# A graph attention layer on one core: scores a group earlier, exponents in three buffers, copied weights in two

## The chip, the cores and the metric

The kernel runs on one core of a Trainium2 chip. The metric is the time of one execution on the device in microseconds; of the kernel before there are three runs, 1566.85 to 1569.98 us, and one profiled execution.

## What is computed

x is 4096 x 128. Four layers of a graph network follow each other, each as x = x + layer(relu(layernorm(x)), adj), with one adjacency matrix of 4096 x 4096 that is almost empty. The change touches the last layer alone:

```python
attn = jnp.einsum('nhc,mhc->hnm', q, k) / np.float32(np.sqrt(C))     # H = 4 heads, C = 32
neg = jnp.where(adj == 0.0, -jnp.inf, attn)
m = jnp.max(neg, axis=-1, keepdims=True)
e = jnp.exp(neg - m)                                                 # 0 where all are masked
alpha = e / jnp.sum(e, axis=-1, keepdims=True)
out = jnp.einsum('hnm,mhc->hnc', alpha, v)
out = beta * x_r + (1.0 - beta) * out                                # beta: a gate from out and x_r
```

## The kernel before

The first layer's pass over the adjacency matrix lists, for every tile of 128 rows, the columns that aren't empty. The other layers work on *groups* of 128 rows and 512 such columns (`Quad`): group q has its buffer b = q % 6 and its turn in a loop that is written out six times (`each_quad`, L369 to L375). The last layer runs 48 groups; a group of another row tile is rescaled and added by an online softmax (`cap`, `capped3`).

For a group, these steps are made, each by one engine:
- SP (`load_adj`, L502 to L516) loads the list, the mask and the queries of group g+5, once DVE has read all scores of group g-1.
- POOL (`gather_nodes`, L685 and L695 on) gathers 512 rows of keys and values in four indirect DMAs for group g+5, once the values of group g-1 are done: `pool.wait_ge(pv_done[k], g.q + 2)`, where the semaphore starts at 2.
- PE turns the keys (`turn_rows`, L1706), 4 transposes; ACT copies them (`keys`, L878) to one buffer kT.
- PE makes the scores (`scores`, L1716): four products of 32 rows each, one a head, into PSUM banks 1 to 4. DVE masks them and takes the maxima (`scores`, L1380, then `maxima3`, L1388 to L1390).
- ACT makes the exponents (`exps3`, L893), four instructions, one a head, in place in `e`.
- PE turns the exponents (`turn_exps`, L1725) in four chunks c of 128 columns, four transposes a chunk; even chunks into bank 5 and copied by ACT (`turned3`, L899), odd ones into bank 6 and copied by DVE (`turned3`, L1396), to `eT`.
- PE multiplies by the values (`values`, L1735): 16 products into bank 7, which show as 32 records and as many weight loads; the last one raises `pv_done`.
- ACT copies the result (`outputs3`, L905), once `pv_done` says so; PE turns it back (`turn_outputs`, L1742); DVE rescales the sum and adds (`add_up3`, L1408 to L1413).

Nothing but the order written in each engine's `step3` decides what runs when. An engine works in order, so a step that waits holds all behind it. In step g PE makes: chunks 2 and 3 of group g, scores of g+2, values of g, chunks 0 and 1 of g+1, keys of g+3, outputs of g. `e` has two buffers and `eT` one. Ahead of the loop stand the first groups' steps (L1753 on for PE); behind it DVE waits for the last exponents and then finishes the layer (`finish3`).

## Time and profile before

| | before |
|---|---|
| median of 3 runs | 1568.05 us (1566.85 to 1569.98) |
| profiled execution | 1554.0 us, span 1552.3 us |
| busy in the span | PE 65%, DVE 58%, POOL 50%, ACT 49% |
| mean granted clock of TensorE | 0.815 of full speed |
| last layer's loop | from about 1176 to 1511 us of the span |

The busy shares are means over four layers with different limits; only the last fifth of the span is in question here. Matmul ends are modelled, so the moment at which a product is really done is read from the engine that waits for it. "remote" and "issue" name waits for which the profile has no other engine's instruction.

### The profile page before, as it was taken

How to read it: one execution, taken by the hardware profiler on the slowest of the kernel's cores; microseconds unless marked ns; L12 is line 12 of the kernel's file. 1: busy time of each engine (PE TensorE's matmuls, PEld its weight loads, DVE VectorE, ACT ScalarE, POOL GpSimd, SP SyncE). 2: the span in 40 equal slices, each digit the busy share in tenths (PEclk: the TensorE clock that was granted, in tenths of full speed). 3: DMA queues.
4: the chain of work that ended last, by engine and by line, in shares of the span. 5: the costliest groups of instructions: out<-in, count | busy, mean ns of one | idle time of the engine just before them, and what ended most of it. 6: DMA issues, size and time to landing. Idle time of an engine off the chain costs nothing.

```text
span 1552.3 us, 29120 instructions
## 1 busy us (share of the span) xinstructions
PE 1006.1 (65%) x6426; PEld 631.8 (41%) x6426; DVE 895.8 (58%) x2430; ACT 756.1 (49%) x3228; POOL 768.8 (50%) x791
## 2 busy tenths in 40 slices
PE   4696858888974515545554286981746777777770
PEld 1353524544542314434443243441524554555440
DVE  3494855986886235544555750103436777777778
ACT  4997666678741313323333250000625666676762
POOL 3007766764555256555655505665054555555550
PEclk9797979898986556665766688996868999999995
DMA  8546656874512444554445876855242445333462
GB/s 272 194 192 227 223 182 180 257 230 166 208 40 64 122 129 101 104 100 94 109 104 98 95 245 224 301 186 62 82 134 79 106 97 105 97 105 100 101 89 58
DMA packets 124455, 219.73 MB, mean 142 GB/s; under 512 B 37350, under 2 KB 93290, under 8 KB 118762
## 3 DMA queue, kind: packets, MB, share of 16 engines
q0 software_dynamic: 25984, 60.45, 21.8%
q1 hardware_dynamic: 83050, 74.24, 15.4%
q10 hardware_dynamic: 15360, 84.43, 14.3%
q14 instruction: 47, 0.39, 0.1%
q8 instruction: 14, 0.23, 0.1%
HBM read 182.18 MB, written 33.18 MB: 139 GB/s over the span
## 4 chain that ended last, share of the span: by engine, by line
DVE 30%; issue 22%; PE 18%; another core or an unknown queue 13%; DVEq 6%; ACT 3%; DMA 3%; SPq 1%; ACTq 1%
DVE work L1380 4%; DVE work L1114 4%; PE ps L1673 3%; PE ps L1716 3%; DVE work L1115 2%; PE ps L1725 2%; PE ps L1526 2%; DVEq L418 1%; DVE work L1051 1%; DVE work L1048 1%; DVE work L1396 1%; DVEq L322 1%; DMA work<-adj_table 1%; PE ps L1522 1%
## 5 line engine op out<-in xcount | busy, mean ns | idle before, releaser
L685 POOL DMA_INDIRECT work<-h_table,stage x304 | 290.6, 956 | 258.8 <-issue 124.9
L801 ACT ACTIVATE unread<-work 128x128 bf16<-128x128 f32 x1024 | 301.0, 295 | 40.8 <-DVE work L1119 16.5
L685 POOL DMA_INDIRECT work<-kv_table,stage x212 | 201.5, 951 | 222.3 <-PE ps L1735 120.5
L642 POOL DMA_INDIRECT work<-in_adj_rows,adj_stage x184 | 238.4, 1296 | 82.6 <-issue 57.0
L1568 PE MATMUL ps<-work,h_wide 128*128 128x512 f32 x512 | 248.5, 641 | 25.5 <-ACT h_wide L732 18.3
L801 ACT ACTIVATION_READ_ACCUMULATOR unread<-work 128x1 f32 x1024 | 191.5, 187 | 7.3 <-issue 6.9
L1380 DVE CUSTOM_DVE_ANT_0 work<-ps,work 128x512 f32<-128x512 f32 x200 | 141.7, 748 | 76.5 <-remote 40.9
L1568 PEld LDWEIGHTS ps<-work,h_wide 128*128 128x128 f32 x512 | 103.7, 208 | 153.7 <-issue 144.8
L1725 PE MATMUL ps<-ident,work 128*128 128x128 f32 x776 | 116.9, 284 | 43.5 <-DVE work L1396 25.1
L893 ACT ACTIVATE work<-work 128x512 f32<-128x512 f32 x197 | 139.8, 713 | 3.5 <-DVE work L1389 2.9
L1648 PE MATMUL ps<-work 128*128 128x128 f32 x384 | 85.9, 394 | 68.9 <-ACT work L842 52.3
L1725 PEld LDWEIGHTS ps<-ident,work 128*128 128x128 f32 x776 | 86.6, 143 | 64.8 <-DVE work L1396 34.7
L1735 PE MATMUL ps<-work 128*32 128x128 f32 x1536 | 79.2, 277 | 49.0 <-issue 48.6
L1648 PEld LDWEIGHTS ps<-work 128*128 128x128 f32 x384 | 75.0, 291 | 78.3 <-ACT work L842 40.8
L1550 PE MATMUL ps<-work 128*32 128x128 f16 x1024 | 67.8, 419 | 49.9 <-DVE work L1051 44.4
L633 POOL COPY adj_stage<-adj_flat 128x4 int32 x46 | 20.8, 452 | 157.6 <-issue 145.2
L1673 PE MATMUL ps<-work,h_wide 128*128 128x512 f32 x192 | 90.9, 614 | 6.4 <-issue 5.1
L1641 PE MATMUL ps<-ident,work 128*128 128x128 f32 x192 | 42.9, 363 | 75.3 <-ACT work L830 40.8
L1735 PEld LDWEIGHTS ps<-work 128*32 128x32 f32 x1536 | 49.1, 109 | 103.4 <-issue 99.3
L1246 DVE TENSOR_REDUCE work<-ps 128x1 f32<-128x512 f32 x49 | 33.9, 692 | 84.3 <-remote 56.6
L1396 DVE COPY work<-ps 128x512 f32<-128x512 f32 x97 | 66.7, 688 | 15.7 <-issue 10.0
L829 ACT ACTIVATE work<-work 128x1 f32<-128x1 f32 x49 | 9.9, 203 | 133.7 <-DVE work L1250 83.9
(216 smaller groups left out, 1802.4 us busy)
## 6 DMA issues: line engine op xcount, KB each, us to landing
work<-in_adj_rows ACTq DMA_DIRECT2D x38, 2048.0 KB
work<-adj_table SPq DMA_DIRECT2D x76, 256.0 KB
work<-in_adj_rows SPq DMA_DIRECT2D x6, 2048.0 KB
adj_table<-work SPq DMA_DIRECT2D x96, 128.0 KB
mask_table<-work SPq DMA_DIRECT2D x53, 128.0 KB
work<-mask_table SPq DMA_DIRECT2D x53, 128.0 KB
work<-h_table,stage POOLq DMA_INDIRECT x304
kv_table<-work SPq DMA_DIRECT2D x32, 128.0 KB
```

The source lines that it names most:

```text
L642: nc.gpsimd.indirect_dma_start(out=ag[:, h, c, :], out_offset=None, in_=adj_rows, in_offset=bass.IndirectOffsetOnAxis(ap=adj_stage[:, h // ...
L685: nc.gpsimd.indirect_dma_start(out=rows[:, b, c, :], out_offset=None, in_=table, in_offset=bass.IndirectOffsetOnAxis(ap=stage[:, b, c:c + ...
L801: ins = nc.scalar.activation(unread[:, m % (MQ // 2) * TB + t, :], ring[:, q, m, t * P:(t + 1) * P], ACT.Abs, accum_out=seen[:, b, t, q * ...
L893: nc.scalar.activation(e[:, b % 2, h, :], e[:, b % 2, h, :], ACT.Exp, bias=nbest3[:, b, h:h + 1], scale=SCALE, accum_out=part3[:, b, h:h + ...
L1380: nc.vector.tensor_tensor_reduce(out=e[:, b % 2, h, :], in0=ps[:, 1 + h, :], in1=mk[:, b, :], scale=1.0, scalar=capped3[:, b, h:h + 1], op ...
L1396: nc.vector.tensor_copy(eT[:, c, :, :], ps[:, 6, :].rearrange("p (h n) -> p h n", h=H)).then_inc(eT_outd, 1)
L1550: ins = mm(ps[NC * g:NC * g + NC, 7 if j % 2 else 3, 0:P], coded[:, j % 2, 0, :, m], onehot[:, j % 2, :, m], start=(m < 4), stop=(m >= T - 4))
L1568: ins = mm(ps[:, 0, :], h_sb[:, q * MQ + m, :], ring[:, q, m, :], start=(q + m == 0), stop=False)
L1648: ins = mm(ps[:, 4 + b % 4, 0:P], eT[:, c, 0, :], hg1[:, b, c, 0:P], start=(c == 0), stop=(c == QC - 1))
L1673: ins = mm(ps[:, 4 + nb, :], h_sb[:, m, :], ring2[:, q, m % MQ, :], start=(m == 0), stop=(m == T - 1))
L1725: ins = nc.tensor.transpose(ps[:, 5 + c % 2, h * P:(h + 1) * P], e[:, b % 2, h, c * P:(c + 1) * P], ident[:, :])
L1735: ins = mm(ps[C * h:C * h + C, 7, 0:P], kvg[:, b, c, P + C * h:P + C * h + C], eT[:, c, h, :], start=(c == 0), stop=(c == QC - 1))
```

## The change

The scores run three groups ahead instead of two, with head 0 of a fourth; the exponents have three buffers (`e_of`), the copied chunks two (`eT_of`); the chunks are made in the order 1, 0, 3, 2 (`turn_place`). PE waits for each head's bank by itself, not for all four. The semaphore `pv_read` gets two more counts at the start, and waits on it are shifted by as much. The loads of SP and the gathers of POOL stay as they were. Before the loop, one group more is scored. The diff, without its unchanged lines:

```diff
--- before.py
+++ after.py
@@ -178,7 +178,10 @@
...
         e1 = e[:, :, 0, :]
+        e_third = work[:, 18688:20224].rearrange("p (h m) -> p h m", h=H - 1)
+        e_third_last = work[:, 8192:8704]
         eT = work[:, 12800:14848].rearrange("p (c h n) -> p c h n", c=QC, h=H)
+        eT_other = work[:, 6144:8192].rearrange("p (c h n) -> p c h n", c=QC, h=H)
         kT = work[:, 14848:15360]
@@ -299,6 +302,7 @@
...
             primed += [pv_done[k], pv_done[k], pv_read[k], pv_read[k], state_reset[k]]
+        primed += [pv_read[3], pv_read[3]]
         for k in (1, 3):
@@ -413,6 +417,17 @@
...
             eng.wait_ge(ag_full[h], 32 * i + (64 if h % 2 else 32))
+
+        def e_of(g, h):
+            n = g.b % 3
+            if n < 2:
+                return e[:, n, h, :]
+            return e_third[:, h, :] if h < H - 1 else e_third_last
+
+        def eT_of(g):
+            return eT_other if g.b % 2 else eT
+
+        turn_place = {1: 0, 0: 1, 3: 2, 2: 3}
@@ -882,21 +897,21 @@
...
                 act.wait_ge(mx_ready[3], g.q + 2)
-                wait(act, pv_read[3], g.q)
+                act.wait_ge(pv_read[3], g.q + 1)
                 nc.scalar.activation(alpha3[:, g.b, :], grown3[:, g.b, :], ACT.Exp, scale=SCALE).then_inc(al_ready[3], 1)
...
                 act.wait_ge(mx_ready[3], q + 2)
-                wait(act, pv_read[3], q)
+                act.wait_ge(pv_read[3], q + 1)
                 for h in heads:
-                    nc.scalar.activation(e[:, b % 2, h, :], e[:, b % 2, h, :], ACT.Exp, bias=nbest3[:, b, h:h + 1],
+                    nc.scalar.activation(e_of(g, h), e_of(g, h), ACT.Exp, bias=nbest3[:, b, h:h + 1],
                                          scale=SCALE, accum_out=part3[:, b, h:h + 1]).then_inc(e_ready[3], 1)
...
             def turned3(g, c):
-                act.wait_ge(eT_done[3], QC * g.q + c + 2)
-                act.wait_ge(pv_done[3], g.q + 2)
-                nc.scalar.activation(eT[:, c, :, :], ps[:, 5, :].rearrange("p (h n) -> p h n", h=H),
+                act.wait_ge(eT_done[3], QC * g.q + turn_place[c] + 2)
+                act.wait_ge(pv_done[3], g.q + 1)
+                nc.scalar.activation(eT_of(g)[:, c, :, :], ps[:, 5, :].rearrange("p (h n) -> p h n", h=H),
                                      ACT.Copy).then_inc(eT_out[3], 1)
@@ -905,22 +920,25 @@
...
             def step3(g):
+                exps3(g.ahead(1), (0,))
+                rescale(g)
                 turned3(g, 2)
-                exps3(g.ahead(1), (1, 2, 3))
-                rescale(g.ahead(1))
+                exps3(g.ahead(2), (3, 2))
+                turned3(g.ahead(1), 0)
+                keys(g.ahead(4))
+                exps3(g.ahead(2), (1,))
                 outputs3(g)
-                turned3(g.ahead(1), 0)
-                keys(g.ahead(3))
-                exps3(g.ahead(2), (0,))
...
             keys(Quad(0, 1))
-            exps3(Quad(0, 0), range(H))
-            rescale(Quad(0, 0))
+            exps3(Quad(0, 0), (3, 2))
+            keys(Quad(0, 2))
+            exps3(Quad(0, 0), (1, 0))
+            exps3(Quad(0, 1), (3, 2))
             turned3(Quad(0, 0), 0)
-            keys(Quad(0, 2))
-            exps3(Quad(0, 1), (0,))
+            keys(Quad(0, 3))
+            exps3(Quad(0, 1), (1,))
             each_quad(act, step3)
@@ -1367,17 +1385,17 @@
...
-            def scores(g):
+            def scores(g, heads):
                 q, b = g.q, g.b
-                if not isinstance(q, int):
-                    dve.wait_ge(eT_done[3], QC * q - QC + 1)
-                adj_loaded(dve, 3, g, turns3)
-                dve.wait_ge(cap_ready, q + 2)
-                for h in range(H):
+                if 0 in heads:
+                    wait(dve, eT_done[3], QC * q - 2 * QC + 1)
+                    adj_loaded(dve, 3, g, turns3)
+                    dve.wait_ge(cap_ready, q + 2)
+                for h in heads:
                     dve.wait_ge(s_done, H * q + h + 2)
                     settle(dve)
-                    nc.vector.tensor_tensor_reduce(out=e[:, b % 2, h, :], in0=ps[:, 1 + h, :], in1=mk[:, b, :], scale=1.0,
+                    nc.vector.tensor_tensor_reduce(out=e_of(g, h), in0=ps[:, 1 + h, :], in1=mk[:, b, :], scale=1.0,
                                                    scalar=capped3[:, b, h:h + 1], op0=ALU.subtract, op1=ALU.max,
@@ -1391,9 +1409,9 @@
...
             def turned3(g, c):
-                dve.wait_ge(eT_done[3], QC * g.q + c + 2)
-                dve.wait_ge(pv_done[3], g.q + 2)
-                nc.vector.tensor_copy(eT[:, c, :, :], ps[:, 6, :].rearrange("p (h n) -> p h n", h=H)).then_inc(eT_outd, 1)
+                dve.wait_ge(eT_done[3], QC * g.q + turn_place[c] + 2)
+                dve.wait_ge(pv_done[3], g.q + 1)
+                nc.vector.tensor_copy(eT_of(g)[:, c, :, :], ps[:, 6, :].rearrange("p (h n) -> p h n", h=H)).then_inc(eT_outd, 1)
@@ -1412,7 +1430,7 @@
...
                                         ALU.add).then_inc(pv_read[3], 1)
-                dve.wait_ge(pv_read[3], q + 3)
+                dve.wait_ge(pv_read[3], q + 5)
                 settle(dve)
@@ -1468,10 +1486,11 @@
...
             def step3(g):
-                turned3(g, 3)
-                scores(g.ahead(2))
-                maxima3(g.ahead(2))
+                scores(g.ahead(3), (0,))
                 turned3(g.ahead(1), 1)
+                scores(g.ahead(3), (1, 2, 3))
+                turned3(g.ahead(1), 3)
+                maxima3(g.ahead(3))
                 add_up3(g)
@@ -1486,12 +1505,18 @@
...
             for b in range(2):
-                scores(Quad(0, b))
+                scores(Quad(0, b), range(H))
                 maxima3(Quad(0, b))
+            scores(Quad(0, 2), (0,))
             turned3(Quad(0, 0), 1)
+            scores(Quad(0, 2), (1, 2, 3))
+            turned3(Quad(0, 0), 3)
+            maxima3(Quad(0, 2))
             end = Quad(each_quad(dve, step3, turns3), 0)
-            dve.wait_ge(e_ready[3], H * end.q + H + 3)
+            dve.wait_ge(e_ready[3], H * end.q + 2 * H + 1)
+            dve.wait_ge(eT_out[3], 2 * end.q + 2)
+            dve.wait_ge(eT_done[3], QC * end.q + QC + 1)
             settle(dve)
@@ -1706,12 +1731,13 @@
...
-            def scores(g):
+            def scores(g, heads):
                 q, b = g.q, g.b
-                adj_loaded(pe, 3, g, turns3)
-                pe.wait_ge(kT_out, q + 2)
-                pe.wait_ge(s_read, H * q + 1)
-                for h in range(H):
+                if 0 in heads:
+                    adj_loaded(pe, 3, g, turns3)
+                    pe.wait_ge(kT_out, q + 2)
+                for h in heads:
+                    wait(pe, s_read, H * q + h - 2)
                     rows = slice(C * h, C * h + C)
@@ -1722,39 +1748,42 @@
...
                     for h in range(H):
-                        ins = nc.tensor.transpose(ps[:, 5 + c % 2, h * P:(h + 1) * P], e[:, b % 2, h, c * P:(c + 1) * P],
+                        ins = nc.tensor.transpose(ps[:, 5 + c % 2, h * P:(h + 1) * P], e_of(g, h)[:, c * P:(c + 1) * P],
                                                   ident[:, :])
...
                 q, b = g.q, g.b
-                pe.wait_ge(pv_read[3], q + 2)
+                pe.wait_ge(pv_read[3], q + 4)
                 for c in range(QC):
...
                     for h in range(H):
-                        ins = mm(ps[C * h:C * h + C, 7, 0:P], kvg[:, b, c, P + C * h:P + C * h + C], eT[:, c, h, :],
+                        ins = mm(ps[C * h:C * h + C, 7, 0:P], kvg[:, b, c, P + C * h:P + C * h + C], eT_of(g)[:, c, h, :],
                                  start=(c == 0), stop=(c == QC - 1))
...
                 pe.wait_ge(oT_out, g.q + 2)
-                pe.wait_ge(pv_read[3], g.q + 2)
+                pe.wait_ge(pv_read[3], g.q + 4)
                 nc.tensor.transpose(ps[:, 7, P:2 * P], outT[:, :], ident[:, :]).then_inc(o_done, 1)
...
             def step3(g):
-                turn_exps(g, (2, 3))
-                scores(g.ahead(2))
+                scores(g.ahead(3), (1, 2, 3))
+                turn_exps(g.ahead(1), (1, 0))
+                turn_rows(g.ahead(4))
                 values(g)
-                turn_exps(g.ahead(1), (0, 1))
-                turn_rows(g.ahead(3))
+                turn_exps(g.ahead(1), (3, 2))
+                scores(g.ahead(4), (0,))
                 turn_outputs(g)
...
             turns3 = turns_of(pe)
-            for b in range(2):
+            for b in range(3):
                 turn_rows(Quad(0, b))
-                scores(Quad(0, b))
-            turn_rows(Quad(0, 2))
-            turn_exps(Quad(0, 0), (0, 1))
+                scores(Quad(0, b), range(H))
+            turn_exps(Quad(0, 0), (1, 0))
+            turn_rows(Quad(0, 3))
+            turn_exps(Quad(0, 0), (3, 2))
+            scores(Quad(0, 3), (0,))
             each_quad(pe, step3, turns3)
```

PE's loop before: one step, from chunks 2 and 3 (L1725) over the scores (L1716) and values (L1735) to the keys (L1706) and outputs (L1742).

```order
265 L1725 MATMUL ps<-ident,work 128x128 x8
266 L1712 REGISTER_ALU
267 L1713 ISA
268 L1716 MATMUL ps<-work 128x512 x4
269 L1735 MATMUL ps<-work 32x128 x8
270 L1733 REGISTER_ALU
271 L1735 MATMUL ps<-work 32x128 x8
272 L1720 REGISTER_ALU
273 L1723 ISA
274 L1725 MATMUL ps<-ident,work 128x128 x8
275 L1706 MATMUL ps<-ident,work 128x128 x4
276 L1742 MATMUL ps<-ident,work 128x128
```

The values stand right behind the four scores, ahead of the chunks of the next group and the keys.

PE's loop after the change, from the registers behind the scores of heads 1 to 3: chunks (L1751), keys (L1731), values (L1761), chunks, score of head 0 (L1742), outputs (L1768).

```order
319 L1749 ISA
320 L1751 MATMUL ps<-ident,work 128x128 x8
321 L1731 MATMUL ps<-ident,work 128x128 x4
322 L1761 MATMUL ps<-work 32x128 x8
323 L1759 REGISTER_ALU
324 L1761 MATMUL ps<-work 32x128 x8
325 L1749 REGISTER_ALU
326 L1751 MATMUL ps<-ident,work 128x128 x8
327 L1738 REGISTER_ALU
328 L322 ISA
329 L1742 MATMUL ps<-work 128x512
330 L1768 MATMUL ps<-ident,work 128x128
```

Eight turned chunks and four keys have moved between the scores and the values, and one score has been taken from the others and stands behind the values.

DVE's loop after the change, the end of a step: the copy of chunk 3 (L1414), the maxima (L1406 to L1408) and the beginning of the addition (L1426).

```order
958 L1414 COPY work<-ps 128x512
959 L1406 TENSOR_TENSOR work<-work 128x4
960 L1407 TENSOR_SCALAR work<-work 128x4
961 L1408 ISA
962 L1408 TENSOR_SCALAR work<-work,cap 128x4
963 L433 REGISTER_ALU
964 L433 TENSOR_LOAD quad_tile
965 L433 ISA x2
966 L1424 REGISTER_ALU
967 L1426 ISA
968 L1426 TENSOR_TENSOR work<-work 128x132
```

Before, the maxima came ahead of the copy of chunk 1, and the addition behind that; the scores and the copy of chunk 3 stood at the step's beginning.

## Rows read from the trace of the kernel before

**Rows 1.** Windows view of the last layer's loop (start:end; length; busy us of each engine)
```profile
1200.00:1500.00 300.00, 226.10 (x2566) 152.75 (x2565) 218.82 (x671) 205.63 (x547) 159.06 (x169) 0.99 0.45 101
```

**Rows 2.** Timeline of PE: first and last value products (start us, us, engine, line)
```profile
1176.34 0.93 PE L1735 MATMUL ps<-work 128*32 128x128 f32 x21
...
1509.73 1.08 PE L1735 MATMUL ps<-work 128*32 128x128 f32 x32
```

**Rows 3.** Waits view, 1200 to 1500: total us, times, longest
```profile
POOL work L685 <- PE ps L1735: 101.4, 42, 2.7
...
PE ps L1725 <- DVE work L1396: 21.7, 34, 1.6
```

**Rows 4.** Lines view by form, 1200 to 1500: busy us, mean ns | idle before, what ended it
```profile
L1380 DVE CUSTOM_DVE_ANT_0 work<-ps,work 128x512 f32<-128x512 f32 x168 | 119.3, 748 | 43.8 <-remote 32.4 <-PE ps L1716 7.6 <-issue 3.6
...
L1396 DVE COPY work<-ps 128x512 f32<-128x512 f32 x84 | 57.8, 688 | 12.9 <-issue 9.2 <-PE ps L1725 3.0 <-DVE work L1413 0.7
```

**Rows 5.** Timeline of POOL: first and last gathers of two groups
```profile
1306.33 0.95 POOL L685 DMA_INDIRECT work<-kv_table,stage  x1 [2.52 <-PE ps L1735]
...
1310.08 0.94 POOL L685 DMA_INDIRECT work<-kv_table,stage  x1 [0.30 <-issue]
...
1334.59 0.95 POOL L685 DMA_INDIRECT work<-kv_table,stage  x1 [2.36 <-PE ps L1735]
1337.43 0.95 POOL L685 DMA_INDIRECT work<-kv_table,stage  x1 [1.90 <-issue]
...
1339.93 0.95 POOL L685 DMA_INDIRECT work<-kv_table,stage  x1 [0.30 <-issue]
```

**Rows 6.** Timeline of ACT: outputs copy, which waits for the values
```profile
1305.38 0.28 ACT L905 ACTIVATE work<-ps 128x128 f32<-128x128 f32 x1 [1.64 <-PE ps L1735]
...
1312.62 0.28 ACT L905 ACTIVATE work<-ps 128x128 f32<-128x128 f32 x1 [1.66 <-PE ps L1735]
...
1333.80 0.28 ACT L905 ACTIVATE work<-ps 128x128 f32<-128x128 f32 x1 [1.53 <-PE ps L1735]
...
1341.93 0.28 ACT L905 ACTIVATE work<-ps 128x128 f32<-128x128 f32 x1 [2.54 <-remote]
```

**Rows 7.** Timelines of PE and its loads, two groups
```profile
1308.91 1.14 PE L1716 MATMUL ps<-work 32*128 32x512 f32 x8
1309.98 1.06 PE L1735 MATMUL ps<-work 128*32 128x128 f32 x27
...
1312.13 0.46 PE L1735 MATMUL ps<-work 128*32 128x128 f32 x4 [0.46 <-issue]
...
1313.45 0.60 PE L1706 MATMUL ps<-ident,work 128*128 128x128 f32 x4
1313.88 0.27 PE L1742 MATMUL ps<-ident,work 128*128 128x128 f32 x1
...
1309.98 0.80 PEld L1735 LDWEIGHTS ps<-work 128*32 128x32 f32 x28 [0.76 <-issue]
...
1337.28 1.14 PE L1716 MATMUL ps<-work 32*128 32x512 f32 x8
1338.35 1.08 PE L1735 MATMUL ps<-work 128*32 128x128 f32 x32
```

**Rows 8.** Source view of the mask load on SP: duration ns min/median/max
```profile
L514 SPq FUSED_REGOPS  x42: 18/458/704, 1201.9 to 1494.4; - x42
```

**Rows 9.** Timelines of DVE and PE ahead of the first values
```profile
1170.71 0.75 DVE L1380 CUSTOM_DVE_ANT_0 work<-ps,work 128x512 f32<-128x512 f32 x1 [2.06 <-remote]
...
1172.25 0.16 DVE L1388 TENSOR_TENSOR work<-work 128x4 f32<-128x4 f32 x1
...
1172.54 0.68 DVE L1396 COPY work<-ps 128x512 f32<-128x512 f32 x1
...
1174.32 2.09 PE L1716 MATMUL ps<-work 32*128 32x512 f32 x8
```

## The prediction

> **What bounds the kernel now.** The change touches the loop of the last layer alone, so I read that stretch. The windows view gives busy times there: of 300 us PE is busy 226.10, DVE 218.82, ACT 205.63, POOL 159.06 [rows 1]. No engine is full, so waits set the pace. The first value products of the 48 groups start at 1176.34 and the last group's at 1509.73 [rows 2], so a group takes 333.4 / 47 = 7.09 us. The diff suggests that engines wait for each other: PE waits 21.7 us for DVE's copies (L1396) and DVE 7.6 us for score products, over 42 groups [rows 3, 4]. That is 0.7 us a group together. The largest wait is another: POOL waits 101.4 us for the value products (L1735), 42 times, 2.4 in the mean and never over 2.7, and DVE waits 32.4 us for something "remote" in front of its scores [rows 3, 4].
>
> So I laid POOL's gathers beside the end of the value products, which is seen as the start of ACT's L905, since ACT waits for just that. At 1305.38 ACT sees the values of a group done; POOL's four gathers start from 1306.33 to 1310.08; the next values are done at 1312.62. From values to first gather 0.95, three steps of 1.25, and 2.54 from the fourth gather to the next values [rows 5, 6]. The reader should see that the last interval hardly depends on PE: when POOL was late by 1.6 us (second gather at 1337.43 where 1334.59 + 1.25 = 1335.84 was due, fourth at 1339.93), PE had issued the scores at 1337.28 and all 32 value products by 1339.43, and yet the values were done only at 1341.93, 2.00 after the fourth gather [rows 5 to 7]. In the ordinary group PE stops in the middle of the values, with 27 of 32 product records issued, for about a microsecond; it goes on at 1312.13, 2.05 after the fourth gather [rows 7]. SP, which does nothing for PE, slows in the same stretch: its register instruction before the mask load takes 18 ns at best and 458 in the median [rows 8]. I read this as **a hold**: while a group's gathers are in flight, completions of PE's products come through late, and about 2.0 us after the fourth gather starts they are let go. POOL in turn starts the next gathers only once the values are done. That closes a ring: 0.87 (0.95 and 0.79 seen, the latter from 1333.80 to 1334.59) + 3.75 + 2.5 = 7.1 us, the 7.09 measured. Mean by the waits view: the four gathers last 4 x 1.25 - 0.30 = 4.70 and POOL's wait is 2.41, together 7.11 [rows 3, 5].
>
> Of contention the Trainium skill says the opposite (SBUF — State Buffer, "Who interferes with whom"): DMA never contends with a compute engine, and PE never waits on anyone. The trace doesn't agree, as far as completions of PE go, since values and gathers move together [rows 5 to 7]. By that rule there is no hold and the loop is bound by the engines' own waits; that is the third case below.
>
> **The change, part by part.**
> *POOL and its wait.* Nothing moves: gather(g+5) still waits for the values of group g-1, four gathers a group. The ring keeps 0.87 + 3.75.
> *PE's order.* Before: exponents' chunks 2, 3; all four scores; values; chunks 0, 1; keys. Now: scores of heads 1 to 3; chunks 1, 0 of the next group; keys; values; chunks 3, 2; the score of head 0; outputs. The number of products is the same. Four heads issued together take 1.07 us until the values follow (1308.91 to 1309.98) [rows 7], as they use different row groups; a head alone costs one head's two passes, the same 1.07. The split adds 1.07 us of PE a group. PE's own need was 1.07 scores + 1.07 values + 21 transposes (16 of exponents, 4 of keys, 1 of outputs) x 0.11 = 4.4 (0.11: 4 keys from 1313.45 to 1313.88) [rows 7]; it is now 5.5. The ring leaves 7.1, so this lies beside it, but with 1.6 us of slack where there were 2.7.
> The Trainium skill speaks against this part too (TensorE: Matmul & The Clock Gate, "Why this matters for your kernels"): a product of 32 rows alone takes as long as one of 128, and the gain is in running four at once. The trace shows the four at once; that one alone costs as much is my reading of it.
> *DVE's and ACT's order.* The same instructions in another order. The buffers (three for exponents, two for the transposed) remove PE's wait for DVE's copy, 21.7 / 42 = 0.5 us, and DVE's for scores, 0.2 [rows 3, 4]. I cost this at nothing: the ring covers it. PE comes to its values earlier, and the hold is late next.
> *From hold to values done.* This is the term that can change. After the hold the value products still queued behind it must run: 2.54 - 2.05 = 0.5 us [rows 5 to 7]. Lower bound: all have run under cover, as at 1341.93, 2.00 after the fourth gather: -0.5 a group. Upper bound: between the first held score and the last value there now stand also 8 turned chunks and 4 keys (24 loads and products). PE stopped before with 27 products and 28 loads of the values issued [rows 7]; if it stops because only so many instructions may stand behind a held one, with 24 more in front some 24 fewer are issued, which is 3 of the 8 steps of 0.13 (1.07 / 8): +0.4. The nearest row is the ordinary group, which had its values partly queued as the new order will (0); the late group had them all (-0.5), but its scores had come through before its second gather could hold them. From 0 I go a quarter of the way to the upper bound, +0.1: 48 x 0.1 = +4.8 us.
> *Prologue.* Three groups are scored before the first values, not two, and group 1 must be turned too. DVE gets free of the gathers at 1170.71, and the first values start at 1176.34 [rows 2, 9]. Added to that chain: 4 scores x 0.75 + maxima 0.3 = 3.3 on DVE and one score pass on PE, 1.07 at full clock, 2.0 at half, as there (2.09) [rows 9]. Sum 4.4 to 5.4; the turned chunks add 8 x 0.11 = 0.9, and some of all this will find cover. I take +5 (3 to 7).
> *End.* Behind the last values now come copy 3, the maxima and only then the addition: 0.69 + 0.3 [rows 4, 9], +1.
> *Sum:* 4.8 + 5 + 1 = +10.8 us. The profiled execution took 1554.0 us (span 1552.3); it becomes 1564.8. The median of the runs, 1568.05, lies 14 us above it; I add the difference to the median: **1578.9 us**. A measurement of this kernel can tell about 0.2%, 3.1 us.
>
> **The rivals.**
> *1, forecast: the ring holds, values end 2.5 to 2.8 behind the fourth gather.* Chance 0.46; own range 1571 to 1593 (0 to +0.4 a group, which is 0 to +19, and 3 to 8 for both ends).
> *2, the ring holds but the rest behind the hold vanishes.* PE is early enough that all values have run when the hold ends: 2.0 instead of 2.5. -0.5 x 48 + 6 = -18: 1550. For it: 1341.93, with everything issued. Against: there are more completions between. Chance 0.22.
> *3, there is no hold; the engines' waits bound, as the diff supposes.* Then the period falls to the fullest engine plus its gaps: by their busy times over 42 groups [rows 1], ACT 4.9, DVE 5.2, PE 5.4 and 1.07 for the split score, 6.5, less what its records overlap: about 6.2, so -0.9 x 48 + 6 = -37: 1531. For it: PE's and DVE's waits above. Against: the values that kept to the gathers [rows 5 to 7]. Chance 0.10.
> *4, slower by much: the hold costs more marks.* Seven completions of PE (three heads, two chunks, the keys, the values) now fall behind the start of the hold; before it was five. Single ones slip through about 0.7 us apart (SP's step at its worst, 704 ns [rows 8]). If even one more of them has to pass before the values are free, the period grows by 0.7: +34 + 6 = 1608. It decides from the point where PE's queue is full before the chunks are done. Chance 0.12.
> *5, no difference:* the prologue's additions vanish under its gathers, and the tail is as before: 1568 to 1571. Chance 0.10.
>
> **Numbers.** Faster by over 0.2%: all of 2 and 3, 0.32, and 0.01 of 5: 0.33. Within: 0.05 of case 1 and 0.08 of case 5: 0.13. Slower: the rest, 0.54. The range, 1540 to 1602, takes in 1, 2 and 5 with their bounds and the nearer part of 4; outside are 3 and most of 4.
>
> **What would show it.** Right: POOL's gathers still in fours 1.25 apart, with the period still 7.0 to 7.5, and L905's twin on ACT starting 2.4 to 2.9 us behind the fourth gather; PE's wait for DVE's copies near zero with no time gained; the first values some 5 us later. Case 2 shows as 2.0 there, case 4 as 3.2. I am wrong at the root if the interval from fourth gather to values falls under 1.9, or POOL's idle time per group under 1.8.

## The result, and the profile after

The changed kernel takes 1638.56 us (median of 4 runs, 1629.14 to 1644.02), the kernel before 1569.01 in the same comparison: ratio 1.0435, interval 1.0375 to 1.0494. The forecast was slower, but by 11 us; it is 70, and outside the range. The profiled execution has a span of 1627.4 us, 75.1 longer than before.

The windows view of the changed kernel, same stretch as [rows 1], has the first surprise: fewer instructions, and a granted clock of 0.89 where it was 0.99.

```profile
1200.00:1500.00 300.00, 241.28 (x2104) 145.86 (x2096) 177.03 (x555) 164.62 (x452) 132.82 (x141) 0.89 0.35 85
```

POOL makes 141 gathers in 300 us and not 169. A period that is evenly longer by 1.4 us would say the same; so I read the timeline of POOL over three groups.

```profile
1427.16 0.94 POOL L700 DMA_INDIRECT work<-kv_table,stage  x1 [2.70 <-PE ps L1761]
...
1434.69 0.94 POOL L700 DMA_INDIRECT work<-kv_table,stage  x1 [2.84 <-PE ps L1761]
...
1442.05 0.94 POOL L700 DMA_INDIRECT work<-kv_table,stage  x1 [2.66 <-PE ps L1761]
...
1457.49 0.94 POOL L700 DMA_INDIRECT work<-kv_table,stage  x1 [10.74 <-PE ps L1761]
```

It is not even. Most groups take 7.0 to 7.5 us, waits of 2.7 to 2.8 against 2.4 before; every sixth takes 13.0 to 15.5, with a wait of up to 11.8. Six groups are one turn of the written-out loop. The waits view, 1220 to 1520, names others than before [rows 3]: DVE is idle 59.1 us ahead of its scores for "issue", which is nothing that the profile shows, 8.0 at the longest, and PE then waits for DVE's copy, up to 5.7.

```profile
POOL work L700 <- PE ps L1761: 134.2, 33, 11.8
...
DVE work L1398 <- issue: 59.1, 28, 8.0
...
PE ps L1751 <- DVE work L1414: 29.6, 10, 5.7
```

What DVE does there stands in the chain of waits, 1436 to 1458 (start, us, what); L376 is the branch at the loop's end, and what follows it at the head:

```profile
1438.34 0.04 DVEq L376
1438.41 0.07 DVEq L376
1438.48 4.08 issue
1442.55 0.09 DVEq L376
1442.64 0.05 issue
1442.69 0.18 DVEq L412
1442.87 2.16 issue
1445.03 0.04 DVEq L1394
```

DVE branches back and stands still for 4.08 us, runs two instructions and stands still for 2.16 more. The profile shows no semaphore for either: before the change DVE's next instruction came 0.3 us behind its branch, and behind the branches of PE, ACT and POOL it still comes within 0.3 us, behind SP's within 0.8. The part of the profile on the queues has what DVE waits for. Whole kernel, before and then changed:

```profile
q14 instruction: 47, 0.39, 0.1%
```

```profile
q14 instruction: 82, 0.67, 0.1%
```

Packets of this kind carry code: 35 more of 8 KB, five for each of the seven branches back. Between the first turn and the last group of the loop before there is none; between 1260 and 1500 of the changed kernel there are 24:

```profile
q14 instruction: 24, 0.20, 0.3%
```

In the raw records of one turn they start at 1439.67, 1439.98, 1443.17, 1445.90 and 1468.02: two in the first stand-still, one in the second, then ahead of need. From 1445.90 to 1468.02 DVE runs 126 instructions. The profile doesn't name the engine of a queue; that q14 is DVE's I take from these times.

Behind the stand-still comes a second price. PE was idle for 5.7 us, and the windows 1446 to 1450 and 1450 to 1455 show a granted clock of 0.50, the lower of its two levels (1.2 GHz); by 1455 to 1460 it is back at 0.98. How much of a turn's price is the stand-still and how much the clock, no run separates.

```profile
1441.00:1446.00 5.00, 0.06 (x2) 0.00 (x0) 0.69 (x3) 2.36 (x8) 3.04 (x4) 0.90 0.22 64
1446.00:1450.00 4.00, 3.27 (x10) 2.07 (x10) 3.57 (x14) 1.13 (x2) 0.74 (x1) 0.50 0.24 66
1450.00:1455.00 5.00, 5.00 (x17) 2.65 (x17) 2.30 (x7) 0.98 (x4) 0.00 (x0) 0.50 0.15 40
1455.00:1460.00 5.00, 5.00 (x55) 2.83 (x53) 3.76 (x13) 4.74 (x13) 1.90 (x3) 0.98 0.16 41
```

The source view of the outputs' copy on ACT gives the layer in three parts (first and last start), before (L905) and changed (L920):

```profile
L905 ACT ACTIVATE work<-ps x48: 277/277/278, 1177.6 to 1513.8; 128x128 f32<-128x128 f32 x48
```

```profile
L920 ACT ACTIVATE work<-ps x48: 265/275/277, 1188.0 to 1588.6; 128x128 f32<-128x128 f32 x48
```

From the layer's first gather (1135.6 and 1140.9) to the first outputs 42.0 became 47.1; the 47 periods 336.2 became 400.6; the end 38.5 became 38.8. So +5.1, +64.4 and +0.3; the rest of the 75.1, 5.3, lies ahead of the layer, which the change doesn't touch.

### The profile page after: what moved, and what is told of

Read it like the earlier page. It is cut to its first block, busy times and chain, and to the rows that moved or that the text cites. A ratio compares the mean times of both kernels' runs of the same rounds, so it can differ in the third digit from the quotient of the medians.

```text
span 1627.4 us, 29399 instructions
## 1 busy us (share of the span) xinstructions
PE 1098.3 (67%) x6448; PEld 672.3 (41%) x6448; DVE 895.2 (55%) x2442; ACT 750.2 (46%) x3232; POOL 774.0 (48%) x791
## 4 chain that ended last, share of the span: by engine, by line
PE 28%; issue 16%; DVE 15%; another core or an unknown queue 10%; DVEq 4%; DMA 2%; ACT 2%; ACTq 1%; POOL 0%; SPq 0%; POOLq 0%
PE ps L1742 6%; PE ps L1751 6%; PE ps L1698 3%; PE ps L1761 2%; PE ps L1551 2%; DVEq L433 1%; DVE work L1398 1%; DVE work L1264 1%; PE ps L1666 1%; DMA h_table<-h_wide 1%; PE ps L1731 1%; PE ps L1593 1%; DMA h_table<-h_t 1%; DVE work L1253 1%
## 5 line engine op out<-in xcount | busy, mean ns | idle before, releaser
L1673 PE MATMUL ps<-work 128*128 128x128 f32 x384 | 89.9, 408 | 90.0 <-ACT work L857 65.3
L1751 PE MATMUL ps<-ident,work 128*128 128x128 f32 x784 | 121.9, 304 | 37.7 <-DVE work L1414 35.3
L1742 PE MATMUL ps<-work 32*128 32x512 f32 x410 | 130.4, 745 | 19.8 <-ACT work L893 10.5
L914 ACT ACTIVATE work<-ps 128x512 f32<-128x512 f32 x97 | 57.9, 597 | 170.9 <-remote 103.6
L1751 PEld LDWEIGHTS ps<-ident,work 128*128 128x128 f32 x784 | 95.4, 154 | 93.1 <-issue 52.0
L648 POOL COPY adj_stage<-adj_flat 128x4 int32 x46 | 27.2, 591 | 152.3 <-issue 135.2
L1414 DVE COPY work<-ps 128x512 f32<-128x512 f32 x98 | 67.5, 689 | 54.1 <-PE ps L1751 30.5
L1761 PE MATMUL ps<-work 128*32 128x128 f32 x1536 | 69.7, 286 | 35.7 <-issue 33.7
L1666 PE MATMUL ps<-ident,work 128*128 128x128 f32 x192 | 45.3, 379 | 59.4 <-ACT work L845 30.3
L857 ACT ACTIVATE work<-ps 128x512 f32<-128x512 f32 x48 | 28.7, 597 | 118.8 <-remote 100.8
```

What stands on the lines that cost most here:

```text
L1673: ins = mm(ps[:, 4 + b % 4, 0:P], eT[:, c, 0, :], hg1[:, b, c, 0:P], start=(c == 0), stop=(c == QC - 1))
L1742: mm(ps[:, 1 + h, :], qs[rows, b, :], kT[rows, :], start=True, stop=True).then_inc(s_done, 1)
L1751: ins = nc.tensor.transpose(ps[:, 5 + c % 2, h * P:(h + 1) * P], e_of(g, h)[:, c * P:(c + 1) * P], ident[:, :])
L1761: ins = mm(ps[C * h:C * h + C, 7, 0:P], kvg[:, b, c, P + C * h:P + C * h + C], eT_of(g)[:, c, h, :], start=(c == 0), stop=(c == QC - 1))
```

## The experiments

**Theory A.** DVE keeps a few blocks of code of 128 instructions (8 KB) and fetches what it no longer has. The built program has 258 instructions in DVE's loop before, 261 now, and 1331 ahead of it before, 1350 now. Two instructions run between the stand-stills, so the loop's head lies at place 126 of a block, and its end at 126 + 260 = 386, three instructions into a fourth block (128 x 3 = 384). Before it began at 126 - 19 = 107 and ended at 107 + 257 = 364, within three. **Rival B**: the new order waits at the turn for data. **Rival C**: the ordinary groups' 7.3 us come from the fetches too.

**e1.** Eight waits for something long done, ahead of the loop, where DVE is idle:

```diff
+            for n in range(8):
+                dve.wait_ge(post_done[3], T)
+                settle(dve)
             turns3 = turns_of(dve)
```

> The changed kernel with eight instructions that only wait for something long done put on DVE before the last layer's loop, where DVE is idle; nothing else differs. Theory A (code of DVE): the loop of 261 instructions lies over four blocks of 128 in the changed kernel, its last three instructions in the fourth; the code of its head is then gone at each turn, is fetched anew, and DVE stands still for 4.1 and 2.3 us, seven times. Shifted by eight it lies over three blocks: the groups of 13 to 15 us vanish, about 7 x 7 = 49 us, 1580 to 1595 us, with no fetch of code between 1230 and 1550. Rival B (the new order waits at the turn for data or a semaphore): nothing changes, 1630 to 1645 us. Rival C (the period of the undisturbed groups, 7.3 us, is caused by the fetches too): the period falls back to 7.1 and the time to about 1578.

Measured: 1585.19 us, ratio 1.0053 (1.0019 to 1.0087) to the kernel before. 53 us are gone by adding instructions; on one chip it is 54.5 (e14 and e15, 1641.37 and 1586.84). No group takes over 8.4 us, the clock is 1.00, and the page counts 48 packets of code, where the kernel before had 47:

```profile
1200.00:1500.00 300.00, 257.05 (x2491) 155.52 (x2489) 206.57 (x650) 189.71 (x526) 154.08 (x163) 1.00 0.41 99
```

```profile
q14 instruction: 48, 0.39, 0.1%
```

B falls, and C too: without fetches the mean period is still 7.35, not 7.1.

**e10 and e11.** The same with one wait and with two, to find the edge.

> The changed kernel with one idle wait ahead of DVE's loop. By the trace its loop's first instruction lies at place 126 of a block of 128 and the last at 386 - 256 = 130 places further on, in the fourth block; with one more it lies at 127, still over four blocks. Theory A: as slow as the changed kernel, with five fetches of code a turn, 1630 to 1650 us. A theory in which any shift helps: about 1585.

> The same with two idle waits: the loop's first instruction lies at place 0 of the next block, its 261 instructions over three blocks. Theory A: no fetches at the turns, 1578 to 1593 us, 50 us faster than with one wait. A theory in which the padding must be larger, or another effect of place: 1630 to 1650.

Measured: 1643.1 us with one (two runs), 1590.34 with two, ratios 1.0402 (1.0281 to 1.0522) and 1.0067 (1.0001 to 1.0133). One idle instruction is worth 53 us. With one wait the page has 83 packets of code; in the chain of waits the first stand-still now has one instruction behind it and not two, as the count wants:

```profile
1293.27 4.32 issue
1297.59 0.09 DVEq L376
1297.67 3.08 issue
1300.75 0.18 DVEq L412
```

With two waits the page has 47 again.

**e2 and e3.** The other way round: the kernel before made to cross, and its control. Two idle waits a group in DVE's step (270 instructions), 14 ahead of the loop (head at 107 + 14 = 121) or 34 (13).

```diff
                 maxima3(g.ahead(2))
+                for n in range(2):
+                    dve.wait_ge(post_done[3], T)
+                    settle(dve)
```

> The kernel before, with two such idle waits a group on DVE in the loop (270 instructions instead of 258) and 14 ahead of it, so that by the count of instructions the loop lies over four blocks of 128. Theory A: each of seven turns stalls by some 6 to 7 us as in the changed kernel, 1610 to 1622 us. Rival B (it is the change's order): no difference to the kernel before but for 12 idle waits a turn beside other work, 1566 to 1574 us.

> The same loop of 270 instructions in the kernel before, with 34 idle waits ahead of it instead of 14, so that it lies over three blocks. Theory A: no code is fetched at the turns, 1566 to 1574 us. A theory in which the length of the loop by itself decides: as with 14 ahead, 1610 to 1622 us.

Measured: 1602.02 us, ratio 1.0153 (1.0072 to 1.0235), and 1580.18, ratio 1.0009 (0.9971 to 1.0048). With more instructions in all, the one that lies in three blocks costs nothing. The page of the crossing one has

```profile
q14 instruction: 82, 0.67, 0.1%
```

and that of the other 47. In the raw records of the crossing one seven instructions stand between the two stand-stills, as the count wants (121 + 7 = 128). So it is place, not length or order. The size I had too high: 22 us instead of 45. By the traces a turn costs 4 us there (mean period 7.95 against 7.37, times 47 / 7) and 7.8 in the changed kernel (400.6 against 345.7 in e1, over 7). DVE stands still nearly as long there (raw records, means of seven turns: 3.99 and 1.91 us, against 4.25 and 2.15 in the changed kernel); what covers it in the old order I didn't separate.

**Theory R**, on which the forecast stood: values done, four gathers, a hold that ends 2.0 us after the fourth, values done. **Rival S**: the engines' waits set the period, and gathers follow.

**e4.** POOL gathers for g+4 and waits for the values of g-2: `pool.wait_ge(pv_done[k], g.q + 1)`, `gather(g.ahead(4))`.

> The kernel before, in which POOL in step g gathers for group g+4 instead of g+5 in the last layer, and so waits for the values of group g-2 instead of g-1. Theory R (ring: values done, gathers, values done about 2.5 us after the fourth): POOL waits no longer for the values just made, so the ring is open; the period falls from 7.1 to the pace of the engines, 5.5 to 6.5 us, 1510 to 1545 us, unless gathers that follow each other more densely hold PE's completions all the time: then the period stays near 7 and POOL is nearly always busy. Rival S (engines' waits among PE, ACT and DVE set the period, the gathers only follow): the period stays 7.1, 1565 to 1572 us, with POOL's wait unchanged in length but for another group.

Measured: 1575.98 us, ratio 0.9991 (0.9949 to 1.0033), period 7.2, gathers as before, 0.8 us behind the values. It tells nothing, and the expectation was badly thought out: gathers for g+4 behind the values of g-2, or for g+5 behind those of g-1, are both gathers for j+6 behind values j. POOL runs one step ahead in its program and is where it was.

**e5 and e6.** Only two of the four gathers of a group are made, in the kernel before and in the shifted changed one; the other half of each buffer keeps old data.

```diff
-                    for c in range(QC):
+                    for c in range(2 if k == 3 else QC):
```

> The kernel before, in whose last layer only two of the four gathers of a group are made (left out: the keys and values of rows 256 to 511 of a group, so two buffers' halves hold old data; before the loop ten gathers fewer, some 12 us). Theory R (a ring of values, gathers and a hold that ends about 2 us after the last gather): the period is no longer 0.87 + 3.75 + 2.5 but 2.5 us less, under the pace of the engines, and falls to that, 5.5 to 6.3 us: 48 x 0.8 to 1.6 plus 12, 1490 to 1530 us. Rival S (the waits among PE, DVE and ACT set the period and the gathers merely follow the values): the period stays at 7.1, only the 12 us ahead of the loop go: about 1560 us.

> The same halving in the changed kernel, with the eight idle waits ahead of DVE's loop. It shows what the new order is worth where the gathers don't bind. Theory R with the deeper buffers' benefit: PE's waits for copies are gone but it has 1.07 us more of scores a group; the period comes to 5.6 to 6.3 us, within 10 us of the kernel before with halved gathers. If the deeper order is truly better for the engines: 0.5 us a group less than the kernel before with halved gathers, 24 us. If the lone score costs its full time: 0.3 to 1 us a group more, 15 to 50 us slower than it. Rival S: period still 7.3.

Measured: 1501.41 us, ratio 0.9484 (0.9395 to 0.9574), and 1525.12, ratio 0.9684 (0.9598 to 0.9769). S falls. In the kernel before with two gathers, POOL and ACT show a period of 5.8 to 6.2, and the values end 3.8 us after the last gather, not 2.5: the ring no longer binds.

```profile
1340.73 0.95 POOL L685 DMA_INDIRECT work<-kv_table,stage  x1 [3.74 <-PE ps L1735]
1341.99 0.94 POOL L685 DMA_INDIRECT work<-kv_table,stage  x1 [0.31 <-issue]
1346.56 0.95 POOL L685 DMA_INDIRECT work<-kv_table,stage  x1 [3.62 <-PE ps L1735]
```

And where the ring doesn't bind, the new order is the slower one: mean period 6.24 against 5.94. The windows view, 1220 to 1460, of e5 and of e6:

```profile
1220.00:1460.00 240.00, 194.77 (x2468) 136.42 (x2461) 206.16 (x648) 200.37 (x525) 76.33 (x81) 1.00 0.30 76
```

```profile
1220.00:1460.00 240.00, 227.11 (x2337) 141.61 (x2328) 191.46 (x614) 186.83 (x501) 72.53 (x77) 1.00 0.29 73
```

PE goes from 4.8 busy us a group (194.77 / 240 x 5.94) to 5.9 (227.11 / 240 x 6.24), by 1.1. That is the size of the lone score of head 0; in the changed kernel it takes 1.12 us, and the other three together 1.13:

```profile
1457.59 1.12 PE L1742 MATMUL ps<-work 32*128 32x512 f32 x2
...
1458.90 1.13 PE L1742 MATMUL ps<-work 32*128 32x512 f32 x6
```

**e7.** POOL also waits for the addition of group g-1: `pool.wait_ge(pv_read[k], g.q + 2)`.

> The kernel before, in which POOL also waits until DVE has added the outputs of group g-1, about 3.3 to 4.1 us after the values were seen done, so its gathers start some 3 us later in each group; buffers are five groups deep, so no data is missed. Theory R: where the gathers start, the completions behind them are late: values end 2 to 2.5 us after the fourth gather wherever that is, the period becomes 3 us longer, about 10, and the time 1700 to 1720 us; if the values come through before the gathers start, the time may also fall. Rival S: no change, 1566 to 1574 us, and the values then no longer keep a fixed distance to the fourth gather.

Measured: 1654.97 us, ratio 1.0491 (1.0414 to 1.0569), mean period 8.9. POOL, then ACT's outputs:

```profile
1428.50 0.95 POOL L685 DMA_INDIRECT work<-kv_table,stage  x1 [4.00 <-DVE work L1415]
...
1432.26 0.94 POOL L685 DMA_INDIRECT work<-kv_table,stage  x1 [0.30 <-issue]
1437.19 0.94 POOL L685 DMA_INDIRECT work<-kv_table,stage  x1 [3.99 <-DVE work L1415]
```

```profile
1425.73 0.28 ACT L907 ACTIVATE work<-ps 128x128 f32<-128x128 f32 x1 [3.93 <-remote]
1434.42 0.28 ACT L907 ACTIVATE work<-ps 128x128 f32<-128x128 f32 x1 [4.06 <-remote]
```

The gathers start 2.77 us behind the values where it was 0.8, and the values end 2.16 us after the fourth, at 1434.42. 2.77 + 3.76 + 2.16 = 8.69: the values follow the gathers. They don't wait for their data: the last packet of these four gathers ends at 1435.20 in the raw records, 2.9 us after the fourth starts and behind the values (5.2 at most, over 47 groups), and PE turns these keys two steps later. PE's granted clock was 0.81 to 0.87 in this loop, where it was 0.99 to 1.00 before; what that adds to the period isn't separated. The expectation had 10, as I took the delay for 3 us and it is 2.0, and the rest shrinks as in [rows 5, 6] at 1341.93.

**e8.** All four scores together in the shifted changed kernel: PE's `scores(g.ahead(3), range(H))`, and no `scores(g.ahead(4), (0,))`.

> The changed kernel with the eight idle waits ahead of DVE's loop, in which PE issues all four scores of group g+3 together at the start of a step instead of head 0 at the end of the step before. PE's work falls by one score pass, 1.07 us a group. Theory R (PE has slack under the ring): at most 0.2 us a group, 1575 to 1587 us. Rival: PE's own time is what lengthened the period from 7.1 to 7.35: the period goes back to 7.1 and the time falls by about 10 us. A third: head 0 is scored later, so DVE and the values wait for it: slower by up to 1 us a group, 1630 us.

Measured: 1586.37 us against 1585.19 of e1, each beside its own runs of the kernel before, ratios 1.0056 and 1.0053; mean period 7.38 against 7.35. By e6 the lone score costs PE 1.1 us a group; under the ring it costs the kernel nothing that the runs can tell.

**e9.** Gathers let go by the first score of g+2, which comes out of the hold 0.5 us ahead of the values: `pool.wait_ge(s_done, H * g.ahead(2).q + 2)`.

> The kernel before, in which POOL in step g waits, beside the values of group g-1, for the first score of group g+2. Scores of g+2 are let go at the end of a hold, 0.5 us ahead of the values of group g; so the gathers of a step start one group later in the program, but 0.5 us earlier against the hold, and need nothing that the hold delays further. Theory R: period 0.87 + 3.75 + 1.95 to 2.2 = 6.6 to 6.8 instead of 7.1, 48 x 0.3 to 0.5 = 15 to 24 us faster, about 1550 to 1565 where the kernel before takes 1575; if chunks or keys that used to come through before the gathers are now caught too, the hold holds a second round and the period grows to 8 or more, over 1600. Rival S (no ring): 0 to 0.2%.

Measured: 1720.43 us, ratio 1.0925 (1.0801 to 1.1049), mean period 10.3. The second outcome: POOL starts 2.1 us ahead of the end of the values (1350.45 and ACT at 1352.58), having waited 5.7 us for the score. What used to come through between the values and the first gather is now held too: the two chunks that PE issued at 1351.05 are copied by ACT at 1354.96 and by DVE at 1356.45, the latter 2.2 us after the fourth gather.

```profile
1350.45 0.95 POOL L685 DMA_INDIRECT work<-kv_table,stage  x1 [5.70 <-PE ps L1718]
...
1352.58 0.28 ACT L907 ACTIVATE work<-ps 128x128 f32<-128x128 f32 x1 [2.39 <-PE ps L1737]
...
1354.21 0.95 POOL L685 DMA_INDIRECT work<-kv_table,stage  x1 [0.30 <-issue]
...
1356.45 0.69 DVE L1398 COPY work<-ps 128x512 f32<-128x512 f32 x1 [3.38 <-PE ps L1727]
```

The values here came through between the second and the third gather. So the hold lets single completions pass, and "2.0 us after the fourth gather" isn't true of every one. PE's granted clock in this loop was 0.77 to 0.80; what that adds to the 10.3 us isn't separated.

**e12.** An attempt at a version that beats both: PE's `values(g)` ahead of the chunks of g+1 and the keys, on top of e1.

> The changed kernel with the eight idle waits ahead of DVE's loop, and PE's values of group g moved ahead of the chunks 1 and 0 of group g+1 and the keys of g+4, which the deeper buffers allow. In this kernel the values end 2.7 us after the fourth gather, of which 2.0 is the hold and 0.7 what stands in PE's queue behind it. Theory R: with eight chunk products, four keys and their loads no longer ahead of the values, these end 2.0 to 2.3 us after the fourth gather; the period falls from 7.35 to 6.7 to 7.0, 48 x 0.35 to 0.65 = 17 to 31 us, so 1545 to 1570 where the kernel before takes 1577: faster than both. Rival: the chunks now stand behind the values and are caught by the next gathers, and with them the copies and the next values: period 8 or more, over 1600. Rival S: no change, 1585.

Measured: 1396.95 us, ratio 1.034 (1.0322 to 1.0357), on a chip on which the kernel before takes 1349.89. Its trace has the expected 2.1 to 2.2 us from fourth gather to values (2.17 from 1215.49 to 0.81 ahead of POOL's next, 1218.47) and a mean period of 6.8, yet it is slower. Of the kernel before there is no trace from this chip.

**e13 to e16.** So the kernel before, the changed one, the shifted one and this one, together on one chip.

> The kernel before, unchanged, to have its trace from the same chip as the runs beside it; in the last comparison it took 1350 us, over 200 less than elsewhere, and the kernel with the values first 1397. Theory R: its period is 0.87 + 3.75 + a rest of about 2.5 wherever it runs, 7.1 us, and what differs between chips lies ahead of the last loop. Rival: on the faster chip there is no hold for this order, its period is the engines' own 5.9, and that is why the values-first kernel with its ring of 6.7 was 47 us slower there.

> The changed kernel, unchanged, on the same chip. Theory A: seven turns with fetches of code, about 53 us slower than the shifted one beside it, 4 to 5% over the kernel before, on any chip.

> The changed kernel with the eight idle waits, on the same chip. Theory R: period 7.3 to 7.4, 0.4 to 1% over the kernel before. Rival (no hold on the faster chip): period about 6.2, as with half the gathers, and 20 to 30 us over the kernel before.

> The values-first kernel on the same chip as the three others. Its trace shows values 2.1 us after the fourth gather and a period of 6.7 to 6.8 instead of 7.35. Theory R: it is 25 us faster than the shifted kernel, and 10 to 20 us faster than the kernel before, if that has a period of 7.1 on this chip. Rival: where the kernel before runs at 5.9, this one is some 45 us slower.

Measured: 1581.07, 1641.37, 1586.84 and 1603.14 us; to the runs of the kernel before beside them 1.0044 (1.0005 to 1.0082), 1.042 (1.0335 to 1.0506), 1.0053 (1.0014 to 1.0091) and 1.014 (1.0067 to 1.0214). First, the kernel before measured against itself gives +0.4%; the +0.5% of the shifted kernel is hardly more, and its time alone doesn't tell the two apart. Mean periods: 7.25, 8.65, 7.36 (7.35 in e1), and 7.70 for the values-first one, which on this chip isn't even: many groups take 7.2, others 8.3 to 9.9. From the fourth gather to the values it takes 2.8 us in the median here, and 2.1 on the chip of e12; the granted clock from 1250 to 1500 is 0.92, where the shifted kernel had 1.00. What makes the difference isn't shown. Moving the values forward won nothing here: 16 us slower than the shifted kernel, where 25 faster was expected. The values-first kernel's traces on the two chips differ by 206 us, of which 147 lie ahead of the layer, 17 between its first gather and first outputs and 42 in the loop. The chip of e12 wasn't met again; whether the kernel before has the ring there stays open, and with it why values-first lost 47 us to it.

No version beat the kernel before. The repair that brings the changed kernel back to within 0.5 to 0.7% of it is two or eight idle instructions.

## Why the prediction was wrong, by its own steps

**The step that failed** is "DVE's and ACT's order. The same instructions in another order ... I cost this at nothing". DVE's instructions were not the same: three more in the loop and 19 more ahead of it, mostly the scoring of one group more. Running them costs nothing that the runs can tell. Their places in memory cost 55 us of the 70 (400.6 against 345.7 in e1; 53 by the medians): 7.8 us at each of seven turns, for a loop end that moved into a fourth block. No rival had it: no duration in the profile of before shows how near the edge was, only a count of the loop's instructions does. The profile's hint was the row of code packets: 47 on the page, and none of them between the loop's first turn and its last group. That the forecast had the right sign says little: of the 75 us in the trace, what its own terms name makes up 15 (9.5 in the periods, by e1, 5.1 ahead of them and 0.3 behind).

**The ring** stood in the orders forecast: e5, e6 and e7 move with the gathers, e5 by the size expected, e7 by 1.8 us a group where 3 was. As a rule it is too simple: in e9 the values passed among the gathers, and e16's period isn't the sum that e12's was. Case 3, no hold, is refuted by e7, and the 21.7 us that PE waited for DVE's copies [rows 3] are gone in e1 (1.7 in 280 us) with nothing gained, as forecast:

```profile
PE ps L1754 <- DVE work L1414: 1.7, 9, 0.2
```

**The terms.** *From hold to values*: +0.1 us a group forecast, 0 to +0.4 the bounds. From the fourth gather to the values done it is 2.7 us in e1 and 2.5 before (medians), +0.2; on one chip (e15 and e13) the mean periods are 7.36 and 7.25, +0.1. *Prologue* +5: 42.0 became 47.1, and is 47.1 in e1. *End* +1: 0.3. *PE's order*, a lone score at the price of four: e6's 1.1 and the two rows of 1.12 and 1.13 us; hidden under the ring: e8. Without the code blocks the forecast of +10.8 us would have been near: the shifted kernels (e1, e11, e15) are 5.6 to 10.4 over the kernel before.

**Case 4** forecast 1608 from a completion more a group. The time is nearer to it than to mine, but the mechanism isn't there: in e1, without the fetches, the mean period is 0.2 us longer, not 0.7. Nor does any run show that SP's step of 704 ns, from which the 0.7 came, has to do with PE's completions.

**What I said would show it.** The marker for the values, the start of ACT's outputs copy, doesn't serve in the new order: ACT makes an exponents pass first, so the copy starts 4.0 us after the fourth gather though the values are done at 2.7. The end of POOL's wait had to take its place.

**The Trainium skill** has the rule that I didn't look for (Runtime: NRT & Kernel Launch, "Instruction fetch mechanics"): an engine has a small instruction memory that is filled in blocks, and a taken branch whose target isn't in it stalls for the fetch. The traces agree in kind, with 3.4 to 6.0 us and then 1.7 to 3.1 at a turn (the changed kernel, e2, e10, e14). In the size of a block they don't: the page has blocks of 16 KiB, two of them for DVE, and here q14's packets are of 8 KB, and a loop over three such blocks (24 KB) is kept. It has a memory four times as large for PE; in agreement, PE's loop of some 810 recorded instructions isn't fetched turn by turn: beside q14's there is one packet of code between 1260 and 1500 in the changed kernel, of 16 KB, on q8.

The rule of the Trainium skill that DMA never contends with a compute engine and PE never waits on anyone (SBUF — State Buffer, "Who interferes with whom") doesn't fit e7 either, where the values followed gathers that had been moved by 2 us.

## What to carry to other kernels

When an edit adds even a few instructions to an engine with a long loop, or ahead of it, count the loop's length and its place, and look in the trace for packets of code between turns and for idle time behind the branch; a few idle instructions ahead of the loop move it. An order of work is worth only what the ring that binds lets through; halving the suspected link, as e5 does, shows whether it binds, and improving the others doesn't. And the long wait of an idle engine isn't by itself something to gain: here POOL waits 2.4 us a group, and what its gathers hold back sets the pace.

## What was unexpected of the hardware

- One instruction decides over 53 us: DVE's loop of 261 instructions over four blocks of 128 fetches five packets of 8 KB a turn, over three none. Four blocks would be 32 KB; why the fourth isn't kept as well, no run shows.
- A stand-still of DVE spreads: PE was idle for 5.7 us, and its granted clock was 0.50 from 1446 to 1455, where eight products of turned chunks took 1.97 us instead of 1.09 (1446.72 and 1437.33 on PE's timeline):

```profile
1437.33 1.09 PE L1751 MATMUL ps<-ident,work 128*128 128x128 f32 x8
...
1446.72 1.97 PE L1751 MATMUL ps<-ident,work 128*128 128x128 f32 x8 [5.67 <-DVE work L1414]
```

- PE's completions follow POOL's gathers even if these are moved (e7: values 2.16 us after the fourth gather with a start 2 us later; 2.5 in the ordinary order), though single ones pass among them (e9). With two gathers the values are done 3.8 us after the second, and the gathers no longer set the pace. What in the chip holds the completions isn't shown by any run.
- One chip ran the kernel before in 1350 us, where four others took 1576 to 1580. No run shows why.
